# Linear attention stage rewritten: strips of four heads, value products with turned output, denominators from cumulated keys, retrieval sums on GpSimd

## The chip, the cores and the metric

The kernel runs on one core of a Trainium2 chip. The time is the device time of the execution in microseconds (us), and the figure compared is the median of several executions. A separate execution is recorded by the profiler. Five engines matter here: PE (TensorE; "PEld" is its weight load), DVE (VectorE), ACT (ScalarE), POOL (GpSimd) and SP (which only issues DMAs). They run their own instruction lists in order and meet only at semaphores.

## The reference

The whole program is a small network over `x` of 8 batches, 256 tokens, 128 features. Six stages run one after the other: F1 (time-mix feed-forward), L (linear attention), F2 (feed-forward again), R1 (routed local and heavy attention), A (latent attention), R2 (routed attention again). The change concerns stage L alone, which computes this for each batch (16 heads of 8 features, segments of 32 tokens):

```python
xn = x * rsqrt(mean(x*x) + EPS) * norm_w
q, k, v = xn @ Wq.T, xn @ Wk.T, xn @ Wv.T            # in 16 heads of 8
pq, pk = elu(q) + 1.0, elu(k) + 1.0
# per head, causal over all tokens up to the query's own:
num   = sum over d <= c of (pq[c] . pk[d]) * v[d]
denom = pq[c] . cumsum(pk)[c] + 1e-6
x_out = x + (num / denom) @ Wo.T
# retrieval: softmax over the earlier segments' means and the running mean
attn_w = softmax([u . m_stack (only earlier segments), u . m_current])
h_retrieved = sum over segments n of attn_w[n] * (pq @ S_cum[n])   # 8x8 state per head
out = gate_current * x_out + h_retrieved
```

## The kernel before

A batch is two halves of 128 tokens. Everything is float32. Stage L is `lin_tensor`, `lin_scalar`, `lin_gpsimd` and `lin_vector`: one function per engine, each an order written out by hand, joined by counting semaphores. Before the first batch each engine runs the preparation of that batch; then `batches` runs a body per batch, with the first and last bodies written out and the six between them in a hardware loop of three turns of two bodies. The body of batch b holds the attention of b, the output of b-1 and the preparation of b+1, so the stage is a software pipeline one batch deep.

Preparation: normalise (L307), transpose `y` (`turn_y`), project to q, k, v, u (`project_in`), scale q and k and take exp (`scale_qk`, `exp_phi`, `phi`), transpose phi(q) and phi(k) (`turn_phi`). Then phi(k) is multiplied by 16 head masks into 16 copies `l_pkm`, four on POOL (L757), four on ACT (L718), eight on DVE (L863). POOL also builds the running segment values (`segment_values`, L768), from which `end_states` makes the states after each segment, masked by `keep_states`.

Attention: a batch has 8 units, each one half and four heads. `scores` of a unit is four matmuls (L589), each with all 128 rows of one head's masked keys as the stationary operand and 128 queries moving. `mask` (L868, DVE, 512 columns) applies the causal triangle. `values` of a unit is four matmuls (L604), with the masked 128x128 scores as the stationary operand and only 9 columns moving: 8 of `v` and a column of ones that gives the denominator. Two PSUM banks alternate between units, so unit u+1 is scored while unit u is masked. `divide` divides, `turn_out` transposes the result and `project_out` applies Wo.

Retrieval: `retrieve` multiplies phi(q) with the states, `weigh` (L894, DVE) applies the gates, `retrieved` (L906, DVE) sums over segments, `add_retrieved` adds to x.

## Time and profile before

| | us |
|---|---|
| median of 3 runs | 1096.65 (1094.64 to 1098.15) |
| span of the profiled execution | 1087.7 |
| PE busy in that span | 966.8 (89%) |
| DVE busy | 670.0 (62%) |
| ACT busy | 381.5 (35%) |
| POOL busy | 141.6 (13%) |
| mean granted TensorE clock | 0.930 of 2.4 GHz |

The median is 9.0 us above the profiled span; that difference lies outside the first and the last instruction. Times below are microseconds from the start of the span. Stage L runs from about 43 to 277 us. In the profile, matmuls of float32 appear as two records each ("x8" is four matmuls), their ends are modelled, and consecutive ones overlap: what a matmul costs is the distance between the starts of two groups, not the length of one. Where PE is named "busy" it may be waiting for a weight load.

### The profile page before, as it was taken

To read this page: it belongs to the slowest core of one execution; us is meant where nothing else is said; L and a number is where in the kernel's file an instruction comes from. 1 tells how busy PE (TensorE), PEld (TensorE's weight loads), DVE (VectorE), ACT (ScalarE), POOL (GpSimd) and SP (SyncE) were. 2 spreads that over 40 slices of the span, in tenths; PEclk is the share of its full clock that TensorE was granted. 3 is DMA by queue.
4 is the path that set the end of the run, shared out by engine and by line. 5 is a ranking of instruction groups with operands and counts; after the bars stand their busy time and mean duration, and the time that the engine had idled before them with its cause. 6 is when DMAs were issued, how large, how long until landed. Compare 5 with 4: busy or idle time off the path is not lost.

```text
span 1087.7 us, 23083 instructions
## 1 busy us (share of the span) xinstructions
PE 966.8 (89%) x8840; PEld 698.3 (64%) x8840; DVE 670.0 (62%) x1914; ACT 381.5 (35%) x913; POOL 141.6 (13%) x289
## 2 busy tenths in 40 slices
PE   3499999899559999999999589999879999999997
PEld 3378888788446666667776245555446667667775
DVE  5778787887664565566555456667453665565553
ACT  3321111111333434333332136667623433333332
POOL 5011111110110000000000254350010000000000
PEclk9889898999689999999999569999979999999997
DMA  5000000000000000000000233322000000000000
GB/s 188 0 2 1 2 0 0 0 0 1 0 1 1 1 2 2 2 2 2 1 0 1 60 86 97 82 75 75 3 1 1 2 1 2 2 2 2 10 10 20
DMA packets 13751, 20.07 MB, mean 18 GB/s; under 512 B 1504, under 2 KB 12128, under 8 KB 12256
## 3 DMA queue, kind: packets, MB, share of 16 engines
q1 hardware_dynamic: 13520, 18.67, 5.9%
q8 instruction: 60, 0.98, 0.4%
q10 hardware_dynamic: 144, 0.20, 0.1%
q14 instruction: 27, 0.22, 0.1%
HBM read 14.53 MB, written 4.19 MB: 17 GB/s over the span
## 4 chain that ended last, share of the span: by engine, by line
PE 70%; DVE 13%; issue 10%; ACT 4%; POOL 2%; DVEq 1%; DMA 1%; SPq 0%; POOLq 0%; ACTq 0%
PE bank L1598 6%; PE bank L1659 6%; PE bank L1627 6%; PE bank L1645 5%; PE bank L1685 3%; PE bank L1605 3%; PE bank L604 3%; PE bank L1083 2%; PE bank L1833 2%; PE bank L1828 2%; PE bank L589 2%; PE bank L1104 2%; PE bank L1631 2%; PE bank L1117 2%; PE bank L1803 2%
## 5 line engine op out<-in xcount | busy, mean ns | idle before, releaser
L1398 DVE TENSOR_REDUCE arena<-bank 128x2 f32<-128x512 f32 x128 | 85.0, 688 | 53.3 <-PE bank L1083 52.2
L2166 DVE TENSOR_REDUCE arena<-bank 128x4 f32<-128x768 f32 x64 | 61.3, 958 | 65.6 <-PE bank L1631 65.6
L1221 ACT ACTIVATE arena<-bank 128x512 f32<-128x512 f32 x128 | 74.5, 594 | 51.0 <-PE bank L1104 50.2
L604 PE MATMUL bank<-arena 128*128 128x9 f32 x512 | 66.2, 257 | 13.4 <-DVE arena L929 7.5
L604 PEld LDWEIGHTS bank<-arena 128*128 128x128 f32 x512 | 65.6, 200 | 16.6 <-issue 8.7
L1627 PE MATMUL bank<-arena 64*128 64x192 f32 x512 | 76.2, 374 | 0.0
L1598 PE MATMUL bank<-arena,w_sb 128*128 128x256 f32 x256 | 74.5, 418 | 1.3 <-ACT arena L1924 1.3
L589 PE MATMUL bank<-arena 128*128 128x128 f32 x512 | 72.1, 289 | 0.3 <-DVE arena L863 0.3
L1945 ACT ACTIVATE arena<-bank 128x768 f32<-128x768 f32 x64 | 51.9, 811 | 55.8 <-PE bank L1649 54.1
L589 PEld LDWEIGHTS bank<-arena 128*128 128x128 f32 x512 | 67.1, 203 | 2.8 <-DVE arena L863 0.3
L1645 PE MATMUL bank<-arena 64*128 64x192 f32 x512 | 66.2, 356 | 0.4 <-ACT arena L1945 0.4
L1598 PEld LDWEIGHTS bank<-arena,w_sb 128*128 128x128 f32 x256 | 46.1, 199 | 19.3 <-issue 12.4
L1659 PE MATMUL bank<-arena 128*32 128x192 f32 (+2 forms) x1536 | 54.5, 274 | 1.2 <-DVE x L2181 1.2
L1083 PE MATMUL bank<-arena 72*128 72x256 bf16 x256 | 52.4, 291 | 1.1 <-DVE arena L1398 1.1
L1659 PEld LDWEIGHTS bank<-arena 128*32 128x32 f32 x1536 | 42.2, 109 | 17.1 <-issue 12.6
L2082 POOL TENSOR_TENSOR arena<-arena,c_sb 128x8 bf16<-128x8 f32 x32 | 9.1, 283 | 332.4 <-issue 295.4
L1645 PEld LDWEIGHTS bank<-arena 64*128 64x128 f32 x512 | 38.8, 185 | 21.0 <-issue 12.5
L1104 PE MATMUL bank<-arena 128*128 128x256 bf16 x256 | 49.5, 277 | 0.5 <-ACT arena L1221 0.4
L2137 DVE SCALAR_TENSOR_TENSOR arena<-arena,c_sb 16x256 f32<-16x256 f32 x98 | 46.2, 471 | 2.5
L1627 PEld LDWEIGHTS bank<-arena 64*128 64x128 f32 x512 | 38.5, 184 | 14.1 <-issue 7.3
L868 DVE TENSOR_TENSOR arena<-bank,c_sb 128x512 f32<-128x512 f32 x64 | 43.8, 684 | 2.8 <-PE bank L589 2.8
L1935 ACT ACTIVATE arena<-bank 128x512 f32<-128x512 f32 x32 | 19.1, 597 | 73.1 <-PE bank L1605 73.1
(297 smaller groups left out, 1978.4 us busy)
## 6 DMA issues: line engine op xcount, KB each, us to landing
arena<-q_dram SPq DMA_DIRECT2D x24, 192.0 KB
arena<-k_dram SPq DMA_DIRECT2D x24, 192.0 KB
w_sb<-w_dram SPq DMA_DIRECT2D x2, 1578.5 KB, 11.0
q_dram<-arena SPq DMA_DIRECT2D x24, 64.0 KB, 2.9
k_dram<-arena SPq DMA_DIRECT2D x24, 64.0 KB, 2.1
x<-x_dram SPq DMA_DIRECT2D x4, 256.0 KB, 4.4
out_dram<-x SPq DMA_DIRECT2D x4, 256.0 KB, 2.3
c_sb<-c_dram SPq DMA_DIRECT2D x1, 601.5 KB, 6.5
```

The lines of the kernel that those rows point to most:

```text
L589: ins = pe.matmul(bank[1 + u % 2][:, j * P:(j + 1) * P], l_pkm[parity][:, quad * 4 + j, h * P:(h + 1) * P], l_pqT[parity][:, h * P:(h + 1) ...
L604: ins = pe.matmul(bank[7][:, h * 144 + k * LV:h * 144 + (k + 1) * LV], l_a[:, u % 2, j, :], l_v[parity][:, h * LH + k, :], start=u == 0 an ...
L1083: ins = pe.matmul(bank[s % 2][:, h * T:(h + 1) * T], a_stack[n % 3][0][0:STACK_ROWS, u, h * P:(h + 1) * P], a_stack[n % 3][1][0:STACK_ROWS ...
L1104: ins = pe.matmul(bank[2 + u % 2][:, k * T:(k + 1) * T], a_stack[b % 3][1][:, u, k * P:(k + 1) * P], a_stack[b % 3][0][:, u, :], start=Tru ...
L1221: act.activation(a_pT[:, u % (2 * GROUP), :, :].rearrange("p k t -> p (k t)"), bank[2 + u % 2][:, :], ACT.Exp).then_inc(S["p"], 1)
L1398: dve.tensor_reduce(a_mx[:, i % 2, :, u % GROUP], bank[s % 2][:, :].rearrange("p (h k) -> p h k", h=HALVES), AX_X, ALU.max, negate=True).t ...
L1598: ins = pe.matmul(to[:, j * T:(j + 1) * T], w_sb[:, at:at + P], g_zT[b % 2][:], start=True, stop=True)
L1627: pe.matmul(bank[j][:, h * KEYS:(h + 1) * KEYS], q[rows, pair, h * P:(h + 1) * P], k[rows, pair, h * WIN:h * WIN + KEYS], start=True, stop ...
L1645: pe.matmul(bank[2 + j][:, h * KEYS:(h + 1) * KEYS], k[rows, pair, h * P:(h + 1) * P], q[rows, pair, h * WIN:h * WIN + KEYS], start=True, ...
L1659: ins = pe.matmul(to[u * E_COLS:(u + 1) * E_COLS, out_at:out_at + n], stationary(h, u), g_p[:, 2 * s + u // 2, u % 2, h * KEYS + at:h * KE ...
L1945: act.activation(g_p[:, pair, :, :], two_banks(2)[:, :, 0:SPAN], ACT.Exp).then_inc(S["p"], 1)
L2166: dve.tensor_reduce(g_mx[:, s, :, :, i].rearrange("p h j -> p j h"), two_banks(0)[:, :, 0:SPAN].rearrange("p j (h k) -> p j h k", h=HALVES ...
```

## The change

The change rewrites stage L and leaves the five others alone, apart from a counter of POOL's fills.

- **Scores by strips.** The 128 features are four strips of 32 rows, four heads each. phi(q) is copied four times (`l_pqm`), copy n keeping head n of every strip; ACT makes the copies straight from PSUM. One matmul then takes 32 rows of phi(k) as the stationary operand and 4 x 128 columns of masked queries moving, which gives four heads at once. A batch has four rounds of two such matmuls, into banks 0 and 1. The 16 key copies and their masks on POOL, ACT and DVE go. A round waits for the mask of the round before, since the banks are single.
- **Mask.** Four DVE instructions of 1024 columns take the place of eight of 512.
- **Values.** `l_v` now has a step of 32 columns per head with zeros between, so a 32-column window placed at the right offset holds one head's values in its place of the strip and zeros elsewhere. The values are the stationary operand (128 rows, 32 columns) and the masked scores move (128 columns). The output is already transposed, so `turn_out` and its copy go. A half is 16 matmuls; the four strips write to four different quarters of the partitions of bank 7. `carried` adds the state after the first half with one matmul.
- **Denominators.** `key_sums` cumulates phi(k) over tokens with the causal matrix, `products` (DVE) multiplies by phi(q), `denominators` sums within heads. ACT adds 1e-6, takes Ln and Exp of its negative, POOL applies one Newton step (`correct_inverse`), `divide` is a multiplication by the inverse.
- **Retrieval.** One of the three `weigh` instructions stays on DVE, the other blocks go to ACT as six copies with a scale; the sums move from DVE to POOL (`sum_retrieved`).
- **phi.** elu(q)+1 is formed as max(exp(min(q,0)), q+1), with q+1 from ACT (`add_one`).
- **Loop.** `every_batch` writes all eight bodies out, with no hardware loop in stage L.
- **Fills.** POOL zeroes the two `l_v` buffers at the very start of the program.

The core of the diff:

```diff
+            for b in range(S["first"], S["last"]):
+                body(b, (b - S["first"]) % 2, b == S["first"], b == S["last"] - 1)
...
-                for j in range(4):
-                    ins = pe.matmul(bank[1 + u % 2][:, j * P:(j + 1) * P],
-                                    l_pkm[parity][:, quad * 4 + j, h * P:(h + 1) * P],
-                                    l_pqT[parity][:, h * P:(h + 1) * P], start=True, stop=True)
+                wait(pe, S["a"], b * ROUNDS + k)
+                for n in range(2):
+                    rows = slice((2 * pair + n) * SEG, (2 * pair + n + 1) * SEG)
+                    ins = pe.matmul(bank[n][:, :], l_pkT[parity][rows, h * P:(h + 1) * P],
+                                    l_pqm[parity][rows, :, h * P:(h + 1) * P], start=True, stop=True)
...
-                    ins = pe.matmul(bank[7][:, h * 144 + k * LV:h * 144 + (k + 1) * LV],
-                                    l_a[:, u % 2, j, :], l_v[parity][:, h * LH + k, :],
-                                    start=u == 0 and j == 0, stop=True, skip_group_check=True)
+                for n in range(COPIES):
+                    for r in range(STRIPS):
+                        at = (h * LH + r * COPIES) * VSTEP + n * VWIN
+                        ins = pe.matmul(num_to[r * SEG:(r + 1) * SEG, h * P:(h + 1) * P],
+                                        l_v[parity][:, at:at + SEG], l_a[2 * h + r // 2][:, r % 2, n, :],
+                                        start=h == 0 and n == 0, stop=True, skip_group_check=True)
...
+                denominators(b)
+                retrieve(b, parity)
+                if not first:
+                    project_out(b - 1)
+                if not last:
+                    turn_y(b + 1, 1 - parity)
+                scores(b, 1, parity)
...
+                act.activation(l_pqT[parity][:], bank[6][:, 0:T], ACT.Copy)
+                act.activation(l_pkT[parity][:], bank[6][:, T:2 * T], ACT.Copy)
+                for n in range(COPIES):
+                    ins = act.activation(l_pqm[parity][:, n, :], bank[6][:, 0:T], ACT.Copy, scale=c("strips")[:, n:n + 1])
...
+                act.activation(l_den[:], den_to, ACT.Identity, bias=c("eps")).then_inc(S["rec"], 1)
+                act.activation(l_ln[:], l_den[:], ACT.Ln).then_inc(S["rec"], 1)
+                act.activation(l_raw[:], l_ln[:], ACT.Exp, scale=-1.0).then_inc(S["rec"], 1)
...
+                link(pool.tensor_tensor(l_part[:], l_ret[:, 0:3, :], l_ret[:, 3:6, :], ALU.add))
+                pool.tensor_tensor(l_hret[:, 0, :], l_ret[:, NST, :], l_ret[:, NST + 1, :], ALU.add)
...
+                sum_retrieved(b)
+                correct_inverse(b)
                 if not last:
                     segment_values(b + 1, 1 - parity)
-                    masks(b + 1, 1 - parity)
```

PE's row in the middle of a batch of stage L, before: score units (L589) and value units (L604, 9 columns) alternate with the steps of the preparation of the next batch (L531 the running means, L551 and L556 the retrieval scores, L564 the transposes of phi).

```order
L531 MATMUL bank<-arena,c_sb 128x256
L589 MATMUL bank<-arena 128x128 x4
L596 REGISTER_ALU
L600 MATMUL bank<-arena 128x144
L604 MATMUL bank<-arena 128x9 x4
L551 MATMUL bank<-arena,w_sb 128x8
```

And now (L549 running means, L619 a round of scores, L631 the values of one half, L568 and L573 the retrieval scores, L639 `carried`, L582 the transposes of phi, L589 and L591 `key_sums`, L604 to L608 `end_states`):

```order
L549 MATMUL bank<-arena,c_sb 128x256
L619 MATMUL bank<-arena 128x512 x2
L631 MATMUL bank<-arena 32x128 x16
L568 MATMUL bank<-arena,w_sb 128x8
L573 MATMUL bank<-arena 128x8 x2
L639 MATMUL bank<-arena 128x128
L619 MATMUL bank<-arena 128x512 x2
L582 MATMUL bank<-c_sb,arena 128x128 x4
L589 MATMUL bank<-c_sb,arena 128x256
L591 MATMUL bank<-c_sb,arena 128x128
L604 MATMUL bank<-arena 128x512
```

The transposes of phi, which wait for DVE's `phi`, used to have a unit of scores behind them; now the longest run of matmuls of the batch stands behind them.

POOL's row of one batch, before (L768 `segment_values` of the next batch, L757 the four key copies), with what each waits for:

```order
L768 TENSOR_TENSOR arena<-arena,c_sb 128x512 [waits linear_states,linear_v]
L768 TENSOR_TENSOR arena<-arena,c_sb 128x384
L757 TENSOR_TENSOR arena<-arena,c_sb 128x1024 [waits linear_pT]
L219 UNCONDITIONAL_BRANCH
L219 ISA
```

And now (L819 to L824 `sum_retrieved`, L831 to L834 `correct_inverse`, L808 `segment_values` of the next batch):

```order
L819 TENSOR_TENSOR arena<-arena 128x384 [waits linear_added,linear_ret_used]
L820 TENSOR_TENSOR arena<-arena 128x128 [waits linear_ret_sum]
L821 TENSOR_TENSOR arena<-arena 128x128
L822 TENSOR_TENSOR arena<-arena 128x128 [waits linear_ret_sum]
L823 TENSOR_TENSOR arena<-arena 128x128
L824 TENSOR_TENSOR arena<-arena 128x128 [waits linear_ret_sum]
L831 TENSOR_TENSOR arena<-arena 128x256 [waits linear_rec]
L832 TENSOR_SCALAR arena<-arena 128x256 [waits linear_rec]
L834 TENSOR_TENSOR arena<-arena 128x256 [waits linear_oT,linear_rec]
L808 TENSOR_TENSOR arena<-arena,c_sb 128x512 [waits linear_states,linear_v]
L808 TENSOR_TENSOR arena<-arena,c_sb 128x384
```

`segment_values` of the next batch, which `end_states` on PE waits for, stands behind nine new instructions, the first of which waits for the gates' products of this batch.

## Rows read from the trace of the kernel before

**Rows 1.** Windows: the steady batches of stage L; busy us, records, then clock.

```profile
62.00:272.00 210.00, 196.29 (x1367) 174.81 (x1366) 166.04 (x403) 37.88 (x119) 27.33 (x21) 0.93 0.00 0
```

**Rows 2.** Groups of stage L: line, operation, records | busy, mean ns | idle before.

```profile
L589 PE MATMUL bank<-arena 128*128 128x128 f32 x512 | 72.1, 289 | 0.3 <-DVE arena L863 0.3
L604 PE MATMUL bank<-arena 128*128 128x9 f32 x512 | 66.2, 257 | 13.4 <-DVE arena L929 7.5 <-DVE arena L868 5.9
L868 DVE TENSOR_TENSOR arena<-bank,c_sb 128x512 f32<-128x512 f32 x64 | 43.8, 684 | 2.8 <-PE bank L589 2.8
...
L768 POOL TENSOR_TENSOR arena<-arena,c_sb 128x512 f32<-128x512 f32 (+1 forms) x16 | 16.1, 1026 | 136.6 <-ACT arena L703 136.6
...
L718 ACT ACTIVATE arena<-arena,c_sb 128x256 f32<-128x256 f32 x32 | 13.6, 496 | 0.3
```

**Rows 3.** Timeline: start, us, engine, line; four moments that bound stage L.

```profile
48.09 0.60 DVE L307 TENSOR_SCALAR arena<-x,mean_var,rstd 128x128 f32<-128x128 f32 x2
...
62.52 2.05 PE L589 MATMUL bank<-arena 128*128 128x128 f32 x16 [0.26 <-DVE arena L863]
...
272.64 0.19 DVE L926 TENSOR_SCALAR arena<-bank 128x32 f32<-128x32 f32 x1 [1.15 <-PE bank L604]
...
277.00 0.49 DVE L273 BATCH_NORM_STATS2 stats<-x 128x6 f32<-128x128 f32 x2
```

**Rows 4.** Timeline of PE at full clock: distances between groups of matmuls.

```profile
99.90 1.06 PE L589 MATMUL bank<-arena 128*128 128x128 f32 x8
100.80 0.96 PE L604 MATMUL bank<-arena 128*128 128x9 f32 x8
...
122.51 1.02 PE L614 MATMUL bank<-arena 128*128 128x512 f32 x2
123.37 0.81 PE L615 MATMUL bank<-arena 128*128 128x384 f32 x2
124.01 1.05 PE L589 MATMUL bank<-arena 128*128 128x128 f32 x8
```

**Rows 5.** Timeline of PE in stage R1: matmuls on parts of the array.

```profile
370.42 0.60 PE L1627 MATMUL bank<-arena 64*128 64x192 f32 x4
370.95 0.20 PE L1631 MATMUL bank<-g_neg,g_row 1*128 1x64 bf16 x2
...
371.74 0.87 PE L1659 MATMUL bank<-arena,c_sb 128*32 128x192 f32 x24
372.43 0.85 PE L1659 MATMUL bank<-arena 128*32 128x192 f32 x24
...
374.81 0.52 PE L1645 MATMUL bank<-arena 64*128 64x192 f32 x4
...
375.16 0.24 PE L1649 MATMUL bank<-arena,c_sb 64*128 64x192 bf16 x2
```

**Rows 6.** L863's durations (ns, min/median/max), and the timeline of DVE beside POOL.

```profile
L863 DVE TENSOR_SCALAR arena<-arena,c_sb x64: 338/341/2089, 58.5 to 251.9; 128x256 f32<-128x256 f32 x64
...
58.59 1.89 POOL L757 TENSOR_TENSOR arena<-arena,c_sb 128x1024 f32<-128x1024 f32 x1 [2.84 <-ACT arena L712]
...
101.01 2.01 POOL L768 TENSOR_TENSOR arena<-arena,c_sb 128x512 f32<-128x512 f32 x2 [16.91 <-ACT arena L703]
101.11 1.22 DVE L819 TENSOR_SCALAR arena<-arena 128x512 f32<-128x512 f32 x1
```

**Rows 7.** Timeline: POOL's last fill and its first work of stage F1.

```profile
10.03 1.80 POOL L1294 MEMSET arena<- 64x2048 f32 x1
...
14.11 0.61 POOL L410 TENSOR_TENSOR arena<-arena 128x256 f32<-128x256 f32 x1 [2.28 <-ACT arena L379]
```

**Rows 8.** Windows, as Rows 1: stage R1, a fall of the clock in L, a slow stretch of A.

```profile
348.00:505.00 157.00, 156.19 (x2059) 108.73 (x2060) 94.86 (x267) 60.46 (x114) 8.65 (x27) 1.00 0.01 2
...
107.00:112.00 5.00, 5.00 (x25) 5.00 (x26) 3.60 (x6) 2.86 (x10) 1.89 (x1) 0.50 0.01 2
...
622.00:645.00 23.00, 19.50 (x67) 9.15 (x68) 11.15 (x19) 5.30 (x13) 13.96 (x26) 0.50 0.40 109
```

More of the change, by code:

```diff
@@ L96, in make_constants @@
     put("ones", np.ones((P, P)))
+    put("eps", np.full((P, 1), 1e-6, np.float32))
+    put("strips", (p[:, None] % SEG // LK == np.arange(COPIES)[None]).astype(np.float32))
     picks = np.where(rows < B, NQ, NKV).astype(np.float64)[:, None]
@@ L627, in project_out @@
                 for h in range(HALVES):
-                    ins = pe.matmul(bank[3][:, h * P:(h + 1) * P], l_oT[:, h * P:(h + 1) * P], w("l_o"),
+                    ins = pe.matmul(out_to[:, h * P:(h + 1) * P], l_oT[:, h * P:(h + 1) * P], w("l_o"),
                                     start=True, stop=True)
                 ins.then_inc(S["out_psum"], 1)
-            turn_y(S["first"], 0)
-            cumulative_means(S["first"], 0)
-            project_in(S["first"])
-            turn_means(S["first"])
@@ L636, in lin_tensor @@
-            retrieval_scores(S["first"])
-            turn_phi(S["first"])
-            end_states(S["first"], 0)
-            scores(S["first"], 0, 0)
-            def batch(b, parity, first, last):
-                for u in range(8):
-                    if u + 1 < 8:
-                        scores(b, u + 1, parity)
-                    values(b, u, parity)
-                    if u == 0:
-                        if not first:
-                            pe.wait_ge(S["pT"], b + 1)
-                            turn_out(b - 1)
-                        retrieve(b, parity)
-                    if u == 1:
-                        if not last:
-                            turn_y(b + 1, 1 - parity)
-                        if not first:
-                            pe.wait_ge(S["mx"], b + 1)
-                            project_out(b - 1)
-                    if not last:
-                        if u == 2:
-                            project_in(b + 1)
-                        if u == 3:
-                            cumulative_means(b + 1, 1 - parity)
-                        if u == 4:
-                            turn_means(b + 1)
-                        if u == 5:
-                            retrieval_scores(b + 1)
-                            turn_phi(b + 1)
-                        if u == 6:
-                            end_states(b + 1, 1 - parity)
-                        if u == 7:
-                            scores(b + 1, 0, 1 - parity)
@@ L674, in lin_tensor @@
-            batches(pe, S, batch)
-            turn_out(S["last"] - 1)
-            pe.wait_ge(S["x_done"], S["last"] - 1)
+            first = S["first"]
+            turn_y(first, 0)
+            project_in(first)
+            cumulative_means(first, 0)
+            turn_means(first)
+            retrieval_scores(first)
+            turn_phi(first)
+            key_sums(first)
+            end_states(first)
+            scores(first, 0, 0)
+            def batch(b, parity, first, last):
+                denominators(b)
[5 more added lines that the diff above has]
+                scores(b, 1, parity)
+                if not last:
+                    project_in(b + 1)
+                    cumulative_means(b + 1, 1 - parity)
+                scores(b, 2, parity)
+                values(b, 0, parity)
+                if not last:
+                    turn_means(b + 1)
+                    retrieval_scores(b + 1)
+                carried(b, parity)
+                scores(b, 3, parity)
+                if not last:
+                    turn_phi(b + 1)
+                    key_sums(b + 1)
+                    end_states(b + 1)
+                values(b, 1, parity)
+                if not last:
+                    scores(b + 1, 0, 1 - parity)
@@ L677, in lin_tensor @@
+            every_batch(S, batch)
             project_out(S["last"] - 1)
@@ L739, in prepare @@
                 copy_phi(b, parity)
[L740 removed]
                 exp_gates(b, parity)
+            act.wait_ge(filled, 2)
             prepare(S["first"], 0)
             def batch(b, parity, first, last):
[L746 to L747 removed]
+                invert(b)
+                weigh(b, parity)
                 if not last:
                     prepare(b + 1, 1 - parity)
[L751 to L752 removed]
+            every_batch(S, batch)
         def lin_gpsimd(pool, S, prev):
[L755 to L760 removed]
             def segment_values(b, parity):
@@ L829, in current_scores @@
                 dve.wait_ge(S["v"], b + 1)
-                link, end = chain(dve, S["prep_order"], 7, b, 2, 3)
+                link, end = chain(dve, S["prep_order"], 4, b, 1, 2)
                 for h in range(HALVES):
@@ L874, in keep_states @@
                 dve.wait_ge(S["states"], b + 1)
-                link, end = chain(dve, S["prep_order"], 7, b, 4, 6)
                 bd = c("blockdiag").unsqueeze(1)
@@ L987, in batch @@
                     normalise_gates(b + 1, 1 - parity)
-            batches(dve, S, batch)
+                    products(b + 1, 1 - parity)
+            every_batch(S, batch)
             divide(S["last"] - 1)
```

375 lines of the change are left out of this document (186 added, 189 removed).

## Prediction

> **What bounds the kernel now.** I read the page first (PE busy 89% of the span), then the windows of stage L, its groups by line, the timeline, and last the parts of other stages that run the forms of matmul which the change brings. Only stage L changes, so its length is the whole question. Its first batch is normalised at 48.09, its first scores start at 62.52, its last value matmuls are done at 272.6 and its last statistics end at 277.5 [rows 3]: 229.4 us from the first normalisation, of which 210.1 are eight batches, 26.3 us each. In them PE is busy 196 of 210 us, DVE 166, ACT 38, POOL 27 [rows 1]. PE sets the pace, DVE is next. Two thirds of PE's time is scores and values: 72.1 and 66.2 us [rows 2], 17.3 us a batch. The value matmuls move 9 columns and still cost 0.20 us each, about what 128 columns cost, since the load of 128 weight columns sets them. The granted clock is 0.93 on average, so about a seventh of the stretch ran at 1.2 GHz instead of 2.4.
>
> **PE after the change.** At full clock four matmuls of 128 columns take 100.80 - 99.90 = 0.90 us, 0.225 each; 512 columns take 0.86 and 384 take 0.64 [rows 4]. So 1.68 ns a column, and 256 columns 0.43 by proportion.
>
> - Scores: the trace has no matmul on 32 rows. The nearest are on 64 rows, two of which (four records) write different banks from different row halves: 0.35 us from L1645 to L1649, where two of 192 columns one after the other would be 2 x 0.32 = 0.64 [rows 5]. They ran side by side. In L1627 the same pair took 0.53. A round of two 32-row matmuls of 512 columns is thus between 0.86 (side by side) and 1.72 (in turn). I take 0.86, nearest to L1645; four rounds are 3.4 us where 32 matmuls of 0.225 were 7.2.
> - Values: L1659 has this very form, 128 rows and 32 columns on four quarters. Twelve matmuls (x24), 384 columns to each quarter, take 0.69 us [rows 5]; in turn they would take 2.6. A half is 16 matmuls with 512 columns a quarter: 0.69 x 512/384 = 0.92, two halves 1.8 us, where 32 of 0.20 were 6.5. The other bound is no overlap: 16 x 0.225 = 3.6 a half, 7.2 a batch. It is far from the row of the same form.
> - The rest of the batch: `turn_y` 0.45, `project_in` 2 x 0.43 + 4 x 0.225 = 1.76, running means 0.43, three of 8 columns 0.6, `carried` 0.23, `turn_phi` 0.9, `key_sums` 0.43 + 0.23 = 0.66, `end_states` 0.86 + 2 x 0.64 = 2.14, `denominators` 0.43, `retrieve` 2.14, `project_out` 0.45; together 10.2.
>
> PE's sum is 3.4 + 1.8 + 10.2 = **15.5 us a batch**.
>
> **The other engines.** DVE loses the eight key copies of L863 (eight of at least 0.34 us [rows 6]), the sums of L906, two of three weighings and two of the three steps of the division. A mask of 512 columns takes 0.684 us [rows 2]; the 512 more cost at most as much again, less one start, so 1.2 to 1.37, four about 4.9 where eight were 5.5. DVE had 166/8 = 20.8 us a batch [rows 1]; I count 12.8 now. ACT gets six weighing copies, four query copies at no more than L718's 0.496 [rows 2], three steps of the inverse and `add_one`: 8 us. POOL: 0.61 us for 256 elements [rows 7] and 1.89 for 1024 [rows 6] give 0.18 + 1.67 ns an element, so 384 cost 0.82 and 128 cost 0.40. `sum_retrieved` is 0.82 + 5 x 0.40 = 2.8, `correct_inverse` 3 x 0.61 = 1.8, `segment_values` 16.1/8 = 2.0 as now [rows 2]: 6.7 us. Its TENSOR_SCALAR is in no row; 0.61, or up to three times that, would still leave POOL under 8. No engine but PE is full, but chains are now closer.
>
> **What PE waits for.** I walked one batch along the order in the lists with these durations. PE waits 0.5 us for ACT's copy of y, which stands behind the six weighing copies on ACT and ahead of `project_in`; 0.5 for ACT's copies of the means and of g; 0.3 for `products`, which needs ACT's six copies after `turn_phi`: 1.3 us. These are small differences of long chains; 0 to 2.6 bounds them. That masks are single-buffered costs nothing where work of the next batch stands between two rounds: round, mask and wait are 0.86 + 1.2 + 0.2 = 2.3 us, and the steps between rounds are 1 to 6 us long. Hidden by them, it would cost up to 1.4 a round if they were gone.
>
> One more wait comes from POOL. An L863 takes 341 ns, the longest took 2089, 1.75 more, and L757 of 1.89 us starts just after the first L863 of a batch; L819 beside L768 took 1.22 us and ended 0.3 after POOL's first instruction (101.01 + 1.03) [rows 6]. A DVE instruction with its operands in SBUF stood still while POOL's ran. `phi` reads two SBUF tiles, comes when POOL is in `segment_values`, and `turn_phi` waits for it: up to 2.0 us, and 1.7 in the walk. The bounds are 0 (POOL is through, or DVE first) and 2.0; I take 1.7. The Trainium skill (SBUF — State Buffer, on port sharing) says the pair of ports is an exclusive lock and names this case, a two-input DVE instruction against GpSimd reads; this speaks against moving sums to Pool. By that rule the trace agrees; without it the batch would be 1.7 us shorter.
>
> So a batch is 15.5 + 1.3 + 1.7 = **18.5 us**.
>
> **The clock.** In the old stage the granted clock was 0.5, which is 1.2 GHz, in stretches such as 107 to 112 while PE was busy throughout [rows 8]; before it fell PE had done units of scores and of 9-column values [rows 4]. Stage R1, full of 64-row and 32-column matmuls with PE busy 156 of 157 us, held 2.4 GHz [rows 8]. The new stage takes the forms of its scores and values from R1 and the rest from L, so the loss lies between none and the old one. I take a third: the old one was up to half of 0.14 x 210 = 15 us, the new one 5.
>
> **Drains.** The two forms on parts of the array alternate with full ones six times a batch. 0.53 against 0.35 for the same pair in R1 bounds a switch at 0.2 us; those falling in waits cost nothing. Between 0 and 2.2 us a batch; the pair L1645 is itself such a switch and cost nothing visible, so I take 0 and keep 1 for the range. The Trainium skill (TensorEngine Tiling (Array Packing), Key Properties) says that changing the tiling mode drains TensorE; it gives no price, so the sum would stay within these bounds.
>
> **Ends of the stage.** The first preparation loses L863 ahead of the first scores but gets ACT's copies, and `key_sums` and `end_states` stand before them: 14.4 us becomes 15.5. The last batch has no preparation beside it: 14.5 us from its first scores to the statistics, a walk of mask, values, divide, project, add. The loop that is written out removes branches that no row shows on the path: 0. POOL's two more fills, 1024 elements each at half of 1.80 = 0.9, end at 11.83 + 1.9 = 13.8; L410 started at 14.11 after waiting for ACT [rows 7]. That wait hides them; without it they would cost 1.9.
>
> **Sum.** 15.5 + 7 x 18.5 + 14.5 + 5 = 164.5 us where 229.4 was: 65 us less. On the profiled execution that is 1087.7 - 65 = 1022.7; the median stands 9.0 above its span, so 1096.65 - 65 = **1031.5**.
>
> **Rivals.**
> - Cheaper chains: no wait on POOL's lock and a full clock, 15.5 + 7 x 16.8 + 14 = 147: 1096.65 - 82 = 1014. For it: DVE has 5 us of slack a batch.
> - Row strips in turn, not side by side: four rounds cost 3.4 more, part of it in waits, about 19.5 to 21 a batch: 1041 to 1052. The same price has a chain through POOL (three engines feed it, and `end_states` waits for it) if its instructions take 1.3 to 1.5 times the above. Against it: L1645.
> - Value matmuls not side by side: 5.4 more a batch, 1070. Against it: L1659.
> - Clock low for half of the stage: a batch at 1.2 GHz is 31 us (2 x 15.5, PE filled), so 4 of 8 add 50: 1080.
> - **Slower than before**: the clock stays at 1.2 GHz through the stage. Then 19 + 7 x 31 + 21 = 257 us, 27 more than now: 1124. Stage A at 622 to 645 ran so, with PE busy 19.5 of 23 us [rows 8]. It decides from about 70% of the stage at the low clock. Against it: in stage L it was at 2.4 GHz for six sevenths of the batches, and in R1 throughout.
> - The step does not do what it says: DVE work only moves and PE keeps its sum. The lists exclude it: 64 matmuls a batch of unit form become 8 + 32.
>
> **How the numbers follow.** Chances: forecast, 1016 to 1046, 0.62; cheaper chains 0.08; strips in turn or POOL chain 0.16; values in turn 0.03; half low clock 0.07; low clock throughout or worse 0.04. The range 1013 to 1060 takes in the first three but the outer ends, a little over 8 in 10. A measurement of this kernel can tell about 0.3%, 3 us, from no change. Faster by more: 0.95; within: 0.01; slower: 0.04.
>
> **What would show it.** The start of one batch's first scores to the next: 17.5 to 19.5 us. Two L619 in 0.9 us: side by side; 1.7: in turn. Sixteen L631 in about 0.9. PE before L582 idle 1 to 2 us, released by DVE L881, with L881 longer than 0.7 us beside POOL L808. Granted clock 0.95 or more between the first and last scores. POOL busy 6 to 8 us a batch. It is wrong if PE is idle more than 4 us a batch, or the clock is under 0.85.

## The result and the profile after

The kernel after takes **1015.6 us** (median of four runs, 1014.5 to 1016.2), the kernel before 1095.6 beside it (1092.1 to 1098.2): a ratio of 0.926, 95% interval 0.924 to 0.929, 80 us less. The forecast was 1031.5 with a range of 1013 to 1060, so the sign and the range held, and the time lies 16 us below the forecast, by the cheap end. The profiled run took 1014.48 with a span of 1012.7. Executions more than 1.5% above the fastest of their kernel, at a lower granted clock, are left out of all medians and ranges: one of the run "order alone" (1028.6), and some of the kernel before (up to 1105.0).

The top of its page. TensorE is as busy as before in share; its weight loads, VectorE and the count of instructions fell, ScalarE and GpSimd rose:

```profile
span 1012.7 us, 22063 instructions
PE 896.8 (89%) x8472; PEld 597.8 (59%) x8472; DVE 604.5 (60%) x1736; ACT 406.8 (40%) x993; POOL 170.4 (17%) x355
```

Three windows answer [rows 1] and [rows 8]: stage L from its first scores to its last value matmuls, then the start of the stage behind it, then the stage's head. Columns: stretch, then busy us and records of PE, PEld, DVE, ACT, POOL, then the granted clock.

```profile
63.00:197.00 134.00, 126.77 (x971) 74.42 (x969) 102.80 (x234) 62.74 (x198) 55.83 (x86) 1.00 0.01 1
203.00:216.00 13.00, 7.63 (x29) 6.39 (x30) 6.61 (x20) 5.41 (x13) 1.86 (x4) 0.50 0.00 0
...
43.00:64.00 21.00, 11.77 (x38) 7.90 (x40) 8.38 (x48) 6.54 (x22) 1.83 (x2) 0.67 0.01 1
```

The clock is 1.00 from 63 us to 199, in the last batch's value matmuls, where the old batches had 0.93; it is 0.50 at the start of the next stage. The moments that bound the stage, and its last batch, as [rows 3]:

```profile
49.13 0.60 DVE L310 TENSOR_SCALAR arena<-x,mean_var,rstd 128x128 f32<-128x128 f32 x2
...
63.58 1.13 PE L619 MATMUL bank<-arena 32*128 32x512 f32 x4
...
186.36 1.13 PE L619 MATMUL bank<-arena 32*128 32x512 f32 x4
...
193.26 1.13 PE L619 MATMUL bank<-arena 32*128 32x512 f32 x4 [1.50 <-DVE arena L918]
...
198.21 1.10 PE L631 MATMUL bank<-arena 128*32 128x128 f32 x32 [1.33 <-DVE arena L918]
...
201.81 0.49 DVE L276 BATCH_NORM_STATS2 stats<-x 128x6 f32<-128x128 f32 x2
```

Head 63.58 - 49.13 = 14.45; seven batches 186.36 - 63.58 = 122.8, 17.54 each (18.30 the first, in which TensorE waits 0.81 us for `products` and 0.81 for the copy of y, and 17.41 or 17.42 each of the others); last batch to the end of the statistics 202.30 - 186.36 = 15.9. Together 153.2 us where 229.4 was, 76.2 less. The stage starts 1.04 later (48.09 became 49.13), and the span is 75.0 shorter. So the whole gain is in stage L.

One steady batch of PE, from first scores to first scores, 116.70 - 99.29 = 17.41. What a group costs is the distance to the next start:

```profile
99.29 1.13 PE L619 MATMUL bank<-arena 32*128 32x512 f32 x4
100.35 0.70 PE L597 MATMUL bank<-arena,c_sb 128*128 128x256 f32 x2
...
103.79 1.13 PE L619 MATMUL bank<-arena 32*128 32x512 f32 x4
105.27 1.13 PE L556 MATMUL bank<-arena 128*128 128x256 f32 x4 [0.35 <-ACT arena L708]
...
108.71 1.08 PE L631 MATMUL bank<-arena 128*32 128x128 f32 x32
109.72 0.39 PE L568 MATMUL bank<-arena,w_sb 128*128 128x8 f32 x2
110.38 0.61 PE L573 MATMUL bank<-arena 128*128 128x8 f32 x4 [0.27 <-ACT arena L717]
...
112.30 0.66 PE L582 MATMUL bank<-c_sb,arena 128*128 128x128 f32 x4
112.79 0.60 PE L589 MATMUL bank<-c_sb,arena 128*128 128x256 f32 x2
...
116.70 0.70 PE L619 MATMUL bank<-arena 32*128 32x512 f32 x2
```

A round of scores, L619, takes 1.06 (100.35 - 99.29), half the values, L631, 1.01 (109.72 - 108.71). Two waits stand in it: for the copy of y, L708 (105.27 - 103.79 is 1.48, not 1.06: 0.42), and for the copy of g, L717. The chain of waits shows what is behind the first: ScalarE's six weighing copies, L762 and L765 (start, us, what).

```profile
103.28 0.89 ACT arena L762 x3
104.17 0.77 ACT arena L765 x3
104.94 0.28 ACT arena L708
```

The groups that answer [rows 2]: scores and values, 138 us before, are 53 now. The mask, L918, is 1.8 times as long as L868 was and half as frequent.

```profile
L918 DVE TENSOR_TENSOR arena<-bank,c_sb 128x1024 f32<-128x1024 f32 x32 | 39.1, 1221 | 9.8 <-PE bank L619 9.8
L619 PE MATMUL bank<-arena 32*128 32x512 f32 x128 | 36.1, 640 | 1.5 <-DVE arena L918 1.5
L631 PE MATMUL bank<-arena 128*32 128x128 f32 x512 | 17.3, 276 | 1.3 <-DVE arena L918 1.3
```

### The profile page after: what moved, and what is told of

Same layout as the page of the kernel before. It is cut to its first block, busy times and chain, and to the rows that moved or that the text cites. A ratio compares the mean times of both kernels' runs of the same rounds, so it can differ in the third digit from the quotient of the medians.

```text
span 1012.7 us, 22063 instructions
## 1 busy us (share of the span) xinstructions
PE 896.8 (89%) x8472; PEld 597.8 (59%) x8472; DVE 604.5 (60%) x1736; ACT 406.8 (40%) x993; POOL 170.4 (17%) x355
## 4 chain that ended last, share of the span: by engine, by line
PE 76%; DVE 9%; ACT 5%; issue 5%; POOL 2%; DVEq 1%; DMA 1%; SPq 0%; ACTq 0%; POOLq 0%
PE bank L1624 7%; PE bank L1685 7%; PE bank L1653 7%; PE bank L1671 6%; PE bank L1711 3%; PE bank L1631 3%; PE bank L1107 2%; PE bank L619 2%; PE bank L1859 2%; PE bank L1854 2%; PE bank L1128 2%; PE bank L1657 2%; PE bank L1141 2%; PE bank L1836 2%; PE bank L1829 2%
## 5 line engine op out<-in xcount | busy, mean ns | idle before, releaser
L1653 PE MATMUL bank<-arena 64*128 64x192 f32 x512 | 76.2, 374 | 0.0
L918 DVE TENSOR_TENSOR arena<-bank,c_sb 128x1024 f32<-128x1024 f32 x32 | 39.1, 1221 | 9.8 <-PE bank L619 9.8
L1141 PE MATMUL bank<-arena 128*32 128x256 f32 x512 | 41.9, 389 | 0.1
L1976 ACT ACTIVATE arena<-bank 128x256 f32<-128x256 f32 x32 | 12.3, 384 | 70.8 <-PE bank L1685 70.8
L2184 DVE TENSOR_SCALAR arena<-bank 128x512 f32<-128x512 f32 x32 | 22.1, 692 | 30.5 <-PE bank L1624 30.5
L1711 PE MATMUL bank<-w_sb,arena 128*128 128x128 f32 x256 | 36.5, 286 | 2.2 <-DVE arena L2202 2.2
```

Of the source, the lines that this page charges most:

```text
L1141: ins = pe.matmul(bank[4 + g // 2][j * VCOLS:(j + 1) * VCOLS, (g % 2) * T:(g % 2 + 1) * T], a_v[b % VDEEP][:, u, k, :], a_pT[:, u % (2 * G ...
L1653: pe.matmul(bank[j][:, h * KEYS:(h + 1) * KEYS], q[rows, pair, h * P:(h + 1) * P], k[rows, pair, h * WIN:h * WIN + KEYS], start=True, stop ...
L1711: ins = pe.matmul(bank[7][:, T + h * D:T + (h + 1) * D], turned[:, k % 2, h * P:(h + 1) * P], w_sb[:, at:at + D], start=k == 0, stop=k == ...
```

## Experiments

The whole time of one kernel moves by 0.5 to 8 us from run to run (most for the run "order alone", 1009.9 at a mean granted clock of 0.941 to 1017.8 at 0.934), so small steps are judged by the length of a steady batch, which repeats within 0.02 us in a trace and from trace to trace. It is 17.41 in the kernel after, in both of its traces. The code below is shortened: the lines that only count and wait are left out.

### Is it the array's rows and columns that are used side by side?

**Both strips of a round on the same rows.**

```diff
-rows = slice((2 * pair + n) * SEG, (2 * pair + n + 1) * SEG)
+rows = slice(2 * pair * SEG, (2 * pair + 1) * SEG)
```

> From the kernel after. In a scores round both matmuls read the 32 rows of the same strip (the second strip's scores are left out and the first's are computed twice), so they can't use different rows of the array at one time; columns, banks, masks and all the rest stay. Theory (two strips on different rows run side by side; that is why a round took 1.06 us and not 1.9): a round grows by 0.86 us to 1.8 to 1.9, four rounds by 3.4 a batch; PE had about 1 us of waits a batch in which a little of it can hide, so 3.0 to 3.4 a batch, 24 to 28 us in all: 1039 to 1044 us. Rival (a matmul on 32 rows is simply shorter than one on 128, and the strips follow one another anyway): the round stays at 1.06 us and the time within 2 us of 1015.6.

Measured: 1043.6 us (1043.4 to 1044.5), a batch of 20.40. A round is now 106.42 - 104.52 = 1.90:

```profile
104.52 1.98 PE L619 MATMUL bank<-arena 32*128 32x512 f32 x4
106.42 0.70 PE L597 MATMUL bank<-arena,c_sb 128*128 128x256 f32 x2
```

Four rounds are 4 x 0.85 = 3.4 longer, of which 0.42 filled the wait for the copy of y: 2.99. Shown: strips on different rows run side by side, and that is worth 3.0 us a batch, 21 in seven. Of the 28 us not all is this: the last batch grew from 15.9 to 24.8 us, 3.4 of it by the rounds, and most of the rest because its last two rounds and its values ran at a granted clock of 0.50, which they didn't in the kernel after (values of a half 1.87 us instead of 1.01).

**Both strips on all 128 rows**, again in turn, but in the form of the other matmuls.

```diff
-rows = slice((2 * pair + n) * SEG, (2 * pair + n + 1) * SEG)
+rows = slice(0, P)
```

> From the kernel after. Both matmuls of a scores round use all 128 rows of the array, so they can't run side by side, and there is no change between the forms of 32 and 128 rows any more (the scores are then sums over four strips, not those of one). A round took 1.06 us with two strips side by side, 0.86 of it columns. Theory (the other 0.20 is the array running empty where the row form changes): a round takes 2 x 0.86 = 1.72 without it, 2.6 more a batch where two 32-row matmuls in turn gave 3.0 more: batch 20.05, 1037 us. Rival (the 0.20 has another cause, that stays): a round takes 1.92, a batch 20.4 to 20.8, 1040 to 1043.

Measured: 1028.4 us (1027.8 to 1028.8), a batch of 19.28. One round, between full matmuls, is 108.81 - 107.09 = 1.72, and `turn_phi`, L582 behind a round, is 0.43 where it was 0.49:

```profile
107.09 1.88 PE L619 MATMUL bank<-arena 128*128 128x512 f32 x4
108.81 1.03 PE L556 MATMUL bank<-arena 128*128 128x256 f32 x4
...
116.97 0.60 PE L582 MATMUL bank<-c_sb,arena 128*128 128x128 f32 x4
117.40 0.60 PE L589 MATMUL bank<-c_sb,arena 128*128 128x256 f32 x2
```

The theory held in kind and the time came 9 us under it. A round in turn is 1.91 on 32 rows and 1.72 on 128: the 32-row form costs 0.19 in the round. It also costs the full matmul beside it 0.06 to 0.10 (`denominators` 0.53 became 0.43, the means 0.52 became 0.43, `project_in` 1.86 became 1.76). Neither this nor the 0.42 of the wait had I counted. 2.6 for the columns, less 0.42 of the wait and about 0.35 of neighbours, is the 1.87 measured. The Trainium skill (TensorEngine Tiling (Array Packing), Key Properties) says that changing the mode drains TensorE; the two runs agree, with up to 0.19 us a round beside it. They do not tell how much of the 0.19 is paid for the change and how much by 32-row matmuls wherever they stand: no run has two rounds in a row with nothing to wait for between them. That the full neighbours got shorter too speaks for the change.

**Value matmuls quarter by quarter**, nothing left out.

```diff
-for n in range(COPIES):
-    for r in range(STRIPS):
+for r in range(STRIPS):
+    for n in range(COPIES):
```

> From the kernel after. The two loops of the value matmuls change places: the four matmuls of a quarter of the array now follow one another, then the next quarter's; nothing is left out. Theory (matmuls on different quarters run side by side, those on one quarter don't): of 16 matmuls in a half at most 3 pairs still overlap, so a half takes 13 to 16 times 0.215 = 2.8 to 3.4 us instead of 1.01, a batch 3.6 to 4.8 more, less up to 0.5 hidden in waits: 25 to 36 us in all, 1040 to 1052. Rival (the time of these matmuls is that of loading 32 weight columns and of issue, not of the array): a half stays near 1.0 and the time within 2 us of 1015.6.

Measured: 1036.5 us (1036.2 to 1036.7), a batch of 20.17. A half is 123.84 - 121.45 = 2.39 where it was 1.01:

```profile
121.45 2.46 PE L631 MATMUL bank<-arena 128*32 128x128 f32 x32
123.84 1.13 PE L619 MATMUL bank<-arena 32*128 32x512 f32 x4
```

The rival fell, and my price was too high: sixteen in this order take 0.15 each, not the 0.215 of a matmul of 128 columns. Side by side is worth 2.8 us a batch, 21 us in all, not 25 to 36. Why it isn't 0.215 stays open.

### The loop that is written out, alone

Kernel before, stage L's batches written out on all four engines.

```diff
-batches(pe, S, batch)
+every_batch(S, batch)
```

> From the kernel before, with one part of the change alone: the batches of stage L are written out instead of looped, on all four engines. The prediction took this part at 0: 1095.6, within 2 us. Rival (the loop's ends cost TensorE and VectorE time that no row names but as issue; the four starts of a turn show up to 1.5 to 1.9 us more idle time than other batches, three turns): 5 to 10 us less, 1086 to 1091, which would then be a part of the gain that the prediction put on matmuls.

Measured: 1091.8 us (1088.6 to 1093.3), kernel before 1085.4 to 1100.4 beside it, ratio 0.998, 0.994 to 1.0015. No gain that can be told from none; at most 6 us, where the change gave 80. Its window of stage L is that of [rows 1] but for the clock, and its shortest batch took 26.5 us, where the shortest before was 25.7:

```profile
62.00:272.00 210.00, 197.98 (x1344) 175.67 (x1343) 165.50 (x405) 37.83 (x119) 27.32 (x21) 0.91 0.00 1
```

### The fills, and the kernel after once more

```diff
-pool.memset(l_v[n], 0.0).then_inc(filled, 1)    # GpSimd, first of its fills
+dve.memset(l_v[n], 0.0)                         # VectorE, before x arrives
```

> From the kernel after. The two fills of the value buffers with zeros are done by VectorE before x arrives, when it is idle, instead of by GpSimd ahead of its other fills. Theory (stage F1 starts 1.04 us later in the kernel after because GpSimd's later fills now run beside VectorE's first normalisation, at 12.15 us, which takes 2.24 instead of 1.11 us beside them): that instruction takes 1.1 us again, F1 starts 1.0 earlier, and the time is 1014.6, 1.0 less, at the edge of what five rounds can tell; the trace decides. Rival (F1 starts later for GpSimd's own late start): GpSimd's first work of F1 is earlier than in the kernel after only if its wait for ACT is, so no change.

> The kernel after, unchanged, as the row of comparison for the other runs of this group and for the one that filled the value buffers on VectorE (1012.8 us in another group). 1015.6 within 1. If it is 1013 here, the fills were worth nothing; if it is 1015 to 1016, they are worth 1 to 3.

Measured: 1012.8 us (1010.8 to 1014.6) with the fills moved, 1015.9 (1012.9 to 1017.4) for the kernel after in another group. The traces are clearer. In the kernel after, GpSimd's last fill runs to 13.73, and VectorE's four normalisations beside it take 2.24 us:

```profile
11.93 1.80 POOL L1320 MEMSET arena<- 64x2048 f32 x1
...
12.15 2.24 DVE L310 TENSOR_SCALAR arena<-x,mean_var,rstd 128x128 f32<-128x128 f32 x4
14.03 0.66 PE L340 MATMUL bank<-c_sb,arena 128*128 128x128 f32 x2 [14.03 <-DVE arena L310]
...
15.28 0.61 POOL L413 TENSOR_TENSOR arena<-arena 128x256 f32<-128x256 f32 x1 [1.55 <-ACT arena L382]
```

With the fills on VectorE they take 1.12, and TensorE starts 1.17 earlier:

```profile
12.11 1.12 DVE L310 TENSOR_SCALAR arena<-x,mean_var,rstd 128x128 f32<-128x128 f32 x4
...
12.86 0.66 PE L340 MATMUL bank<-c_sb,arena 128*128 128x128 f32 x2 [12.86 <-DVE arena L310]
```

Stage F1 ends 1.3 us earlier (statistics at 43.15 against 44.48). But in three other traces with the fills on GpSimd it ended at 43.35, for VectorE didn't wait the 1.0 us for L358 (stage F1) that it waits in the kernel after, in the kernel before and here. In those three TensorE's matmuls of this place were twice as fast (L351 to L358 0.44 us, in the kernel after 0.85), though the granted clock stands at 1.00 in all of them. So the step is worth 1.2 at the start of F1 and 1.3 at its end against a trace with the same wait, but only 0.2 against one without it. The rest of the 3 us between the two medians is not shown to be the fills.

### Who waits for GpSimd

In the kernel after `phi`, L881, never waited. The copy of two columns ahead of it did, 0.96 us instead of 0.17, beside the first of the two L808 (1.04 us); and the second L808, on 384 columns, took 1.35 us beside `phi`, which had started 0.02 before it, instead of the 0.83 that it takes where nothing meets it (the run with the sums back on VectorE):

```profile
109.72 0.73 POOL L834 TENSOR_TENSOR arena<-arena 128x256 f32<-128x256 f32 x1
110.41 2.35 POOL L808 TENSOR_TENSOR arena<-arena,c_sb 128x512 f32<-128x512 f32 x2
...
110.51 0.96 DVE L894 COPY arena<-arena 128x2 f32<-128x2 f32 x1
111.39 0.68 DVE L881 TENSOR_TENSOR arena<-arena 128x512 f32<-128x512 f32 x1
```

**phi first.**

```diff
-current_scores(b + 1)
-phi(b + 1)
+phi(b + 1)
+current_scores(b + 1)
```

> From the kernel after. On VectorE phi is put ahead of the current scores and their copy, so it is the first to come near GpSimd's instructions, where now a copy of 2 columns does (0.96 us instead of 0.17). Theory (a VectorE instruction with its operands in SBUF waits while GpSimd's runs, whichever comes second waits): phi, 0.68 us now, takes 1.0 to 1.4, or GpSimd's segment multiplication beside it takes 1.4 instead of 1.0, and the copy of 2 columns loses its wait or a part. The time stays within 1 us of the kernel after, since phi now ends 0.2 us before TensorE comes to it and would end no later. Rival (the wait is only one of the small copies): phi stays at 0.68 and ends 0.7 us earlier, time the same. If phi ended later than now, TensorE would wait in L582 and the batch would grow from 17.41.

Measured: 1015.4 us (1012.6 to 1016.3), a batch of 17.41. Durations, min/median/max in ns; L881 was 678/678/684 and L894 169/967/985:

```profile
L881 DVE TENSOR_TENSOR arena<-arena x8: 693/901/917, 57.6 to 179.6; 128x512 f32<-128x512 f32 x8
...
L894 DVE COPY arena<-arena x8: 169/470/471, 58.8 to 181.0; 128x2 f32<-128x2 f32 x8
```

The wait moved from the copy to `phi` in part, as the theory says, though `phi` stayed below my 1.0. In the kernel after `phi` ends at 112.07 and TensorE comes to L582 at 112.30: the wait delays `phi` by 0.8 us, and 0.2 are left before anyone would notice.

**The retrieval sums back on VectorE.**

```diff
-pool.tensor_tensor(...)   # sum_retrieved, six additions on GpSimd
+dve.tensor_tensor(...)    # the same six, between the last mask and add_retrieved
```

> From the kernel after. The six sums of retrieved parts go back from GpSimd to VectorE, between the last mask and the addition to x: one part of the change undone. GpSimd's busy time a batch falls from 7.3 to 4.0 us, VectorE gets 0.45 + 5 x 0.19 = 1.4 more. Theory (waits for the shared port are hidden in the kernel after, and VectorE has 0.9 us idle at this place only): the state masking and products come 0.5 later and TensorE waits 0.3 to 0.5 a batch for them: 1018 to 1020. Rival (the waits for GpSimd cost the path something): they shrink with GpSimd's work and the batch falls by 0.3 to 0.8 us: 1009 to 1013.

Measured: 1020.9 us (1019.7 to 1023.2), a batch of 18.27. The waits for GpSimd did go (L894's copy, now L880, 0.17 again), but TensorE waits for VectorE in `denominators`:

```profile
119.13 0.70 PE L597 MATMUL bank<-arena,c_sb 128*128 128x256 f32 x2 [0.79 <-DVE arena L956]
```

0.86 a batch, more than the 0.3 to 0.5 I gave it: the six take 114.36 to 116.32, 2.0 us and not 1.4. Having the sums on GpSimd is worth 7 x 0.86 = 6 us of the change by the batches, 5 by the medians of this group (1015.9), waits for the port included.

**One more addition on GpSimd.**

```diff
+pool.tensor_tensor(l_spare[...], l_ret[:, 0:3, :], l_ret[:, 3:6, :], ALU.add)
 link(pool.tensor_tensor(l_part[:], l_ret[:, 0:3, :], l_ret[:, 3:6, :], ALU.add))
```

> From the kernel after. GpSimd adds the 384 retrieved columns once more, to a place that nobody reads: 1.0 us more at the head of its chain in each batch, nothing else. In the kernel after its segment multiplication ends 0.7 us before TensorE comes to the end states. Theory (GpSimd's chain is hidden with 0.7 us to spare): TensorE waits 0.3 to 0.6 us a batch there, batch 17.7 to 18.0, 1018 to 1020 us. Rival 1 (GpSimd sets the batch already): 1.0 more, 18.4, 1023. Rival 2 (more room than the trace shows): no change, 1015.6.

Measured: 1015.7 us (1014.8 to 1016.5), a batch of 17.77. The batch is as the theory says: of 1.0 us more, 0.36 reach TensorE. The whole time is not: 7 x 0.36 = 2.5 us don't show in the medians, which move by as much on their own (the profiled spans are 1014.7 here and 1012.7 in the kernel after). GpSimd's chain had about 0.65 to spare.

### What sets the batch, and a shorter kernel

**Order alone.** ScalarE copies y ahead of the three weighings of the first half, TensorE does `carried` ahead of `retrieval_scores`.

```diff
-weigh(b)      # L762, L765
-copy_y(b + 1)
+weigh(b)      # L762
+copy_y(b + 1)
+weigh_first_half(b)   # L765
...
 turn_means(b + 1)
-retrieval_scores(b + 1)
 carried(b, parity)
+retrieval_scores(b + 1)
```

> From the kernel after, the order alone: on ScalarE the copy of y goes ahead of the three weighings of the first half, on TensorE the carried values go ahead of the retrieval scores. TensorE waits 0.35 to 0.42 us a batch for the copy of y and 0.27 for the copy of g in the kernel after; both should go, and GpSimd's sums start 0.4 later, which leaves its chain 0.1 us late at worst. Theory: batch 16.7 to 16.8 instead of 17.41, seven batches 4.3 to 5 us: 1011. Rival (the batch is a ring of waits in which the next one takes their place, GpSimd's chain or a mask): batch 17.2 to 17.4, 1014 to 1015.6.

Measured: 1015.6 us (1009.9 to 1017.8), ratio to the kernel before 0.925 (0.921 to 0.929), the kernel after's was 0.926; a batch of 17.19. Both waits are gone and a new one stands in `end_states`, for GpSimd's segment values:

```profile
113.26 0.38 PE L591 MATMUL bank<-c_sb,arena 128*128 128x128 f32 x2
113.90 1.12 PE L604 MATMUL bank<-arena 128*128 128x512 f32 x2 [0.26 <-POOL arena L816]
```

The rival held: 113.90 - 113.26 is 0.64 where 0.22 is the work, so 0.42 of the gain went into this wait, and 0.22 a batch remained, 1.5 us in seven, less than these whole times can tell.

**All together.** Order, fills, and in the last batch the third round in banks 5 and 6 with the fourth right behind it.

```diff
+at = 5 if b == S["last"] - 1 and k == 2 else 0
-pe.matmul(bank[n][:, :], ...)
+pe.matmul(bank[at + n][:, :], ...)
```

> From the kernel after, for the shortest time: the order of the run with moved steps, the fills of the value buffers on VectorE before x arrives, and in the last batch, where TensorE waits 1.50 and 1.33 us for masks because both rounds use the same two banks, the third round writes banks 5 and 6, and the fourth follows it without the value matmuls between them. 4.3 to 5 us from the order, 1.1 to 1.3 from the fills, 1.2 to 2.5 from the last batch: 1007 to 1009. Rival (the batch is a ring, as above, and the last batch is bound by VectorE's own work): 1013.

Measured: 1009.6 us (1008.6 to 1011.3), ratio 0.921 (0.918 to 0.925). Its steady batch is 17.20, still with the wait for GpSimd; the last batch went from 15.9 to 13.8, in the middle of what was expected. The time is a little over the 1007 to 1009 expected, since the order gave 1.5 us and not 4.3 to 5.

The trace shows where this wait comes from. `phi` (L894 here) starts 0.02 us before GpSimd's segment multiplication, and the first of the two L821 takes 1.49 us, where it took 1.04 in the kernel after:

```profile
108.75 0.68 DVE L894 TENSOR_TENSOR arena<-arena 128x512 f32<-128x512 f32 x1
...
108.77 2.35 POOL L821 TENSOR_TENSOR arena<-arena,c_sb 128x512 f32<-128x512 f32 x2
```

So here GpSimd stands still for VectorE, 0.45 us, and TensorE is late by about as much: 111.18 - 110.52 is 0.66 from L591 to L604, where 0.22 is the work. In the run "order alone" it is the same (1.47 us). In the kernel after the second L808 stood still for 0.52, hidden by the 0.7 us that its chain had to spare.

**GpSimd's inverse last.** The correction of the inverse is needed only in the next batch's division, the segment values within 3 us.

```diff
 sum_retrieved(b)
-correct_inverse(b)
 segment_values(b + 1, 1 - parity)
+correct_inverse(b)
```

> From the run with all steps moved (1009.6 us, a batch of 17.20, in which TensorE waits 0.26 us for GpSimd's segment multiplication and starts it 0.1 late), one more change of order: on GpSimd the segment values of the next batch go ahead of the correction of the inverse, which VectorE needs only some 8 us later. Theory (GpSimd's chain took the place of the two waits that the new order removed): the wait in the end states goes, a batch is 16.75 to 16.9, seven batches 2.1 to 3.1 us less: 1006.5 to 1007.5. Rival (the earlier multiplication meets VectorE's phi, or another wait is next): a batch of 17.1 to 17.2, 1009 to 1010.

Measured: **1005.2 us** (1003.6 to 1006.6), ratio 0.918 (0.914 to 0.922), somewhat better than the 1006.5 to 1007.5 expected. The two L821 now end as `phi` starts, at 108.3 us, and take 1.83 us together, not 2.35; the first step of the inverse, L844, now meets `phi` and takes 1.18 us instead of 0.73, where nobody waits for it. A batch is 16.67, and no PE row of a steady batch has a wait any more; this is the batch in which TensorE's own work is all:

```profile
110.26 0.38 PE L591 MATMUL bank<-c_sb,arena 128*128 128x128 f32 x2
110.48 1.02 PE L604 MATMUL bank<-arena 128*128 128x512 f32 x2
```

Its window of full batches has PE busy 99%, at full clock:

```profile
64.00:180.00 116.00, 115.15 (x896) 69.56 (x898) 91.94 (x219) 59.77 (x189) 51.23 (x77) 1.00 0.01 1
```

It is 10 us faster than the kernel after, in another group of runs; the two ranges don't touch.

## Why the prediction was right, and where it was off

The sum against the trace: head 15.5, measured 14.45; seven batches 129.5, measured 122.8; last batch 14.5, measured 15.9; clock 5, measured none in the batches. 164.5 against 153.2, 11.3 too much. Behind it 1.2 too little: the fills' 1.0 and 0.2 elsewhere. The remaining 6 are no step of the kernel: "the median stands 9.0 above its span" mixed 1.8 us, which in nearly every run lie between span and time, with the luck of one profiled run, so it does not all lie outside the first and the last instruction; after the change the difference was 2.9. (The last subtraction of the sum gives 1031.65, not 1031.5.)

The batch of 18.5 came out at 17.4 by errors that partly cancel: TensorE's own work 1.2 more, its waits 0.6 less, the lock 1.7 less. Of the signs that the prediction named, clock and GpSimd's share came as said; a round took 1.06 and not 0.9, nearer to side by side than to the 1.7 of in turn; the wait of 1 to 2 us before L582 was not there.

- **TensorE's sum, 15.5: too small by 1.2.** The last experiment has it bare: 16.67. Rounds are 4 x 1.06 = 4.2 (3.4 forecast), values 2.0 (1.8), the rest 10.4 (10.2). "Side by side" was right for both forms, shown by the runs that took it away, and [rows 5] gave its size within 10% for the values.
- **Drains, taken 0: wrong.** 0.19 in each round and 0.06 to 0.10 in most of their full neighbours are some 1.2 a batch, within the bounds of 0 and 2.2 and near the 1 kept for the range. That all of it is the change of form is not separated, as said above. I chose 0 for a pair that "cost nothing visible"; the 0.53 of the same pair, in the same rows, was the better witness.
- **Transposes: mis-sized.** `turn_phi` and `turn_y` were priced as matmuls of 128 columns, 0.9 and 0.45; they measured 0.49 and 0.31. The trace of before had the row, one of two transposes that take 0.25 together:

```profile
95.66 0.41 PE L525 MATMUL bank<-c_sb,arena 128*128 128x128 f32 x2
95.91 0.61 PE L628 MATMUL bank<-w_sb,arena 128*128 128x128 f32 x4
```

- **Waits, 1.3: too large.** The copies of y and g cost 0.42 and 0.32, the products nothing: 0.74, and 16.67 + 0.74 is the batch of 17.41. That these waits are small differences of long chains was right: with both gone, a third one took half of their gain.
- **GpSimd's lock, 1.7: the mechanism was there, the place was wrong.** VectorE does stand still for GpSimd, but 0.8 us in a copy of two columns and 0.3 in L866, not 1.7 in `phi`, and 0.2 us short of TensorE. The walk had `phi` meet a whole `segment_values` and wait; it came just before the second half of it, and it was GpSimd that waited, 0.52 us. That side of the lock the prediction left out, and it was the one that reached TensorE, 0.4 us a batch in the runs with the new order. The Trainium skill (SBUF — State Buffer, Who interferes with whom) names copies and tensor_scalar beside the two-input instruction as what can take the shared ports, and says that issue order decides who blocks; L894, L866, L310, the two L808 and the run with phi first agree with both. I had weighed the two-input case alone. What such a wait costs is set by the slack behind it, 0.2 us behind `phi` and 0.7 behind the segment values here, which only the rows of TensorE show.
- **The clock, 5: wrong in this stage.** It was granted in full from 63 us to 199, in the last batch. In the kernel before, ScalarE's copies of y stand at 70.38, 96.11 and so on to 235.39, six batches in 165.0 us; the two in which the clock stayed full took 25.7 and 26.6. Six of these would be 154 to 159, so the clock had cost some 6 to 11 us in those six. That is below the 15 that the prediction allowed the old stage, and what I carried over of it was wrong. Why the old batches lost it and the new ones don't was not settled: TensorE was busy 93% of the old stretch and 95% of the new, and the loop that was written out alone left the old stretch at 0.91.
- **The last batch, 14.5: too small by 1.4.** The walk hid the masks; the trace shows 1.50 and 1.33 us of waiting, since both rounds use two banks. "Costs nothing where work of the next batch stands between" was right, and the last batch has none.
- **The fills, 0: wrong for a reason I hadn't named.** GpSimd was in time; VectorE wasn't, for it stood still beside the fills.
- **The loop, 0**, held within what can be measured.
- **The other engines** came as counted: VectorE 13.4 us a batch (12.8 forecast), ScalarE 8.2 (8), GpSimd 7.3 (6.7; its addition of 384 columns took 1.00, not 0.82), a mask 1.22 (1.2 to 1.37).

The rival of cheaper chains (no wait on the lock, full clock, 16.8 a batch, 1014) is nearest to what happened, and got 8 in 100. It was right in both its conditions. The batch itself was 17.4, because the drains it also left out came in. That its 1014 is within 2 us of the measured time is luck: its stage was 6 us too short, and the difference of median and span, carried over whole, 6 too long.

## What to carry to other kernels

Price a tiled matmul by its row in the trace, and add the change of form, which showed on both sides of a group; whether groups of one form put together would save it was not tried. A wait that is shown by name is worth its length only if the engine behind it isn't late too: here 0.74 us of waits gave 0.22 until GpSimd's order was changed as well, and then all of it. Where an engine shares work with another through a common port, look at both of them: at the slack of what follows the blocked instruction, and at which of the two starts first. Here `phi`, 0.02 us ahead, made GpSimd stand still, and TensorE wait for it; letting the work with the nearest due time go first took this away. And judge a step of a few us by a distance inside the trace that repeats, not by the whole time.

## What the runs showed of the hardware

- A round of two 32-row matmuls in turn, between full ones, takes 1.91 us, the same round on 128 rows 1.72, and a full group beside it is up to 0.10 shorter then. Side by side the round takes 1.06.
- Float32 transposes of 128 x 128 take 0.12 us, where a matmul of 128 columns takes 0.22.
- Sixteen 32-column matmuls take 1.01 us over four quarters in rotation and 2.39 quarter by quarter.
- VectorE's copy of two columns, 0.17 us alone, takes up to 0.98 beside GpSimd's instruction of two inputs; its normalisations, with one tensor operand, 2.24 instead of 1.12 beside a GpSimd memset.
- It goes the other way too: GpSimd's multiplication of 512 columns takes 1.49 us instead of 1.04, that of 384 columns 1.35 instead of 0.83, where VectorE's `phi`, with two inputs in SBUF, starts 0.02 before it.
- The kernel before differed from run to run by 18 us with its granted clock (1085.4 at 0.935, 1103.2 at 0.914); the kernel after by 4.5 (1012.9 at 0.941, 1017.4 at 0.936).
